# A conditioned attention and selective scan kernel: four exponential buffers, sample 1's projections queued ahead of sample 0's maxima, and a residual product that opens its sum

## The chip, the cores and the metric

The kernel runs on one core of a Trainium2 chip. Its time is the device time of one launch in microseconds, taken over several runs. The engines named below are the TensorE (PE), VectorE (DVE), ScalarE (ACT), GpSimd (POOL) and SyncE (SP, which issues nearly all DMAs). Each engine works through its own list of instructions in order and waits on semaphores for the others.

## What is computed

Two residual layers over x of 8 samples, 256 tokens, 256 channels. The first is attention with 16 heads of 16 channels, its weights modulated by a style vector:

```python
x = x + L0(x, q, k, v, w, u weights, cond)
x = x + L1(x, cond, ...)

# L0: x = layernorm(x * s1); q, k, v = projections, scaled by channel
attn = softmax(q @ k.T * 0.25)            # per head, 256 x 256
out  = (attn @ v) @ W.T * w_dc + v_flat @ U.T * u_dc

# L1: xr, gate = split(x @ W_in.T); xr + cond, causal conv of 4 taps, silu, layernorm -> xn
def step(h, ad, bd, xt, ct):              # 256 steps, state 16 x 512 per sample
    h = clip(h * ad + bd * xt, -10, 10)
    return h, ct @ h
y = ys + D * xn
return (y * silu(gate)) @ W_out.T
```

All inputs and the output are float32.

## The kernel before

The program is one list per engine, written out by hand, with a semaphore for each hand-over. There is no planner: the order in each engine's list is the order of the code.

**Attention.** `sample` on the TensorE runs once per sample b. Q and k are projected channels-first into banks 1 and 2 (`channels_of`, L694), copied out, and split by ScalarE and GpSimd into three bfloat16 parts (L480 to L487, L381, L385). SyncE's `stack` (L249, L259) writes the parts to memory and loads them back stacked, so that one matmul of 96 rows gives a float32-like product. A first pass of matmuls (`max_scores`, L713) gives each head's scores and the VectorE takes their row maxima (L1117). The maxima are transposed (L812), copied to bfloat16 (L514), and sent by a small DMA of the ScalarE's queue (L516) into row 96 of the stacked q. The second pass (`scores`, L723) has 97 rows, so it yields scores minus maxima, and the ScalarE takes exponentials (L522) out of banks 4 to 7, a head each, into `ex`. Heads go in four groups of four. For a group g, `weigh(.., False)` (L740) multiplies with v, `add_tiles` on the VectorE (L1135) adds the two halves of the exponentials into `esum`, and `weigh(.., True)` (L733) sums those over the partitions and raises `pv_done`. `attend` (L1141, L1143) divides for two groups at a time.

On the TensorE a sample's order is: maxima of heads 4 to 15, with the next sample's transposes (L686) and three projections between them at heads 4, 7 and 10; transposes of the maxima; output products of the previous sample (L758); scores 0, v transposes (L704), scores 1, weigh 0, scores 2, sums 0, weigh 1, scores 3, sums 1, weigh 2, sums 2, weigh 3, the next sample's first four maxima (`early_maxima`, which waits for the stacked loads), sums 3. Sample 0 has first its own projections, then four small matmuls L873 whose result the VectorE uses for weight gains (L1161 to L1165, `wgain`), for which the TensorE waits before `sample(0)`.

**Middle.** Input projection, convolution, layer norm, split of xn and of the scan's factors into bfloat16 parts, all by way of memory.

**Scan.** The 256 steps go in 16 tiles of 16, each of four groups of four. For step t one bfloat16 matmul (L951, `u_steps`) gives the increment in bank t % 4, and one VectorE instruction (L1315) adds it to the state and clips. For each group, `y_steps` (L962) contracts four states. The previous tiles' results are finished between them: `tile_transpose` (L972) after group 1, `tile_out` (L983) in two halves after group 3 and after group 0 of the next tile but one, the second half with the residual product x1 times identity (L987). The ScalarE copies y, the transposed y, x1 (`take_x1`, L645) and the output (`take_out`, L653). SyncE loads a tile's operands (L297, L305) when the slot's last increment is done, one tile before they are used, and stores the output (L329).

The lines on which the order rests:

```python
act.wait_ge(s["pv_done"], b * 4 + (g - 1))        # ScalarE, L521, before exp of group g
pe.wait_ge(s["wgain"], 1)                         # TensorE, L876, before sample 0
pe.wait_ge(s[f"ld_k{par}"], turn * 48 + 48)       # TensorE, L772, early_maxima
act.wait_ge(s["o_done"], r)                       # ScalarE, L644, before the copy of x1
```

Of the kernel before, what the change touches and what calls it, by code (L numbers as in the profile page):

```python
# [19 lines left out]
ALU = mybir.AluOpType  # L20
ACT = mybir.ActivationFunctionType
AX = mybir.AxisListType

P = 128
# [43 lines left out]
def build(nc, x_tok, xT, s1_row, condT, w5T, winT, wconv, bconv, ln_row, lnT, wxT, wxdt, wdtT, bdt_row, alog_row,  # L68
          woT, ident_d, mask8_d, out):
    with ExitStack() as ctx:  # L70
# [74 lines left out]
        mT = sb0("mT", [NH, S], BF16)  # L145
        ex = sb0("ex", [P, 2, 4, 512])
        esum = sb0("esum", [P, 2, 4, S])
# [307 lines left out]
        def _(act):  # L455
# [51 lines left out]
            def sample(b, par, last):  # L507
# [9 lines left out]
                for n in range(NH):  # L517
                    g = n // 4
                    act.wait_ge(s["st_done"], b * NH + (n + 1))
                    if n % 4 == 0 and not (isinstance(b, int) and b == 0 and g < 2):  # L520
                        act.wait_ge(s["pv_done"], b * 4 + (g - 1))  # L521
                    nc.scalar.activation(ex[:, g % 2, n % 4, :], bank[4 + n % 4][:, :], ACT.Exp, scale=SCALE)\  # L522
                        .then_inc(s["exp_done"], 1)
                    if n == 3 and not last:
                        take_v(b + 1, 1 - par, isinstance(b, int) and b == 0)
# [140 lines left out]
        def _(pe):  # L666
# [60 lines left out]
            def weigh(b, buf, g, sums):  # L727
# [10 lines left out]
                for t in range(HALVES):  # L738
                    for r in range(4):
                        mm(bank[2 * o][32 * r:32 * r + 32, 0:S],  # L740
                           vp[:, buf, t, 4 * o + r, 2 * par:2 * par + 2, :].rearrange("p a d -> p (a d)"),
                           ex[:, g % 2, r, t * S:(t + 1) * S], start=par == 0 and t == 0,
                           stop=par == 1 and t == HALVES - 1, skip_group_check=True)
# [32 lines left out]
            def sample(b, par, next_turn, first, last):  # L776
# [24 lines left out]
                for n in range(EARLY, NH):  # L801
                    if n == 4:
                        next_qkv(0)
# [64 lines left out]
            channels_of(2, 3, "vt_done")  # L868
            v_tokens(0)

            pe.wait_ge(s["ld_l1"], 16 * 11)
# [94 lines left out]
            def tile_transpose(r):  # L966
# [7 lines left out]
                ins.then_inc(s["yt_done"], 1)  # L974

            def tile_out(r, part):

                if part == 0:
                    pe.wait_ge(s["yg_ready"], r + 1)
                    if r >= 1:  # L980
                        pe.wait_ge(s["ob_ready"], r)
                for c in range(2 * part, 2 * part + 2):
                    mm(bank[7][:, 0:H], yg[:, c, :], wo[:, c, :], start=c == 0, stop=False, skip_group_check=True)  # L983
                if part == 1:
                    pe.wait_ge(s["x1s_ready"], r + 1)
                    for k in range(HT):
                        ins = mm(bank[7][:, k * P:(k + 1) * P], x1s[:, k, :], ident[:, :], start=False,  # L987
                                 stop=k == HT - 1, skip_group_check=True)
                    ins.then_inc(s["o_done"], 1)
# [3 lines left out]
            for i in range(R):  # L993
                for g in range(RG):
# [4 lines left out]
                    if i >= 1:  # L999
                        if g == 1:  # L1000
                            tile_transpose(i - 1)
                        elif g == 3:
                            tile_out(i - 1, 0)
                        elif g == 0 and i >= 2:
                            tile_out(i - 2, 1)
            tile_out(R - 2, 1)
            tile_transpose(R - 1)
            tile_out(R - 1, 0)
# [4 lines left out]
        def _(dve):  # L1013
# [107 lines left out]
            def sample(b, first, last, more):  # L1121
# [9 lines left out]
                def add_tiles(g):  # L1131
                    dve.wait_ge(s["exp_done"], b * NH + (4 * g + 4))
                    if not (first and g < 2):
                        dve.wait_ge(s["pv_done"], b * 4 + (g - 1))
                    v.tensor_tensor(esum[:, g % 2, :, :], ex[:, g % 2, :, 0:S], ex[:, g % 2, :, S:], ALU.add)\  # L1135
                        .then_inc(s["es_ready"], 1)
# [238 lines left out]
```

## Time and profile before

| | |
|---|---|
| median of 3 runs | 683.56 us (683.29 to 688.03) |
| the profiled execution | 684.64 us |
| its span, first to last instruction | 682.8 us |
| busy, share of the span | PE 73%, DVE 72%, ACT 35%, POOL 24% |
| chain that ended last | PE 35%, DVE 28%, ACT 15%, DMA 11% |
| largest lines of the chain | DVE scan step L1315 11%, ACT exponentials L522 8%, PE projections L694 6% |
| mean granted TensorE clock | 0.894 |

The span is the profiled execution's stretch from its first to its last instruction; its own time is 1.84 us more. A busy share is an average over stages of different kind, so it does not say what bounds any of them. The chain of waits is followed back from the last instruction, at each step to what released it. In a timeline row the first number is the start from the span's beginning, the second the time from the first to the last of the instructions that the row merges, x4 their count, and the bracket the engine's idle time ahead of them with what ended it. The granted clock is a share of 2.4 GHz: 0.5 is the lower of its two levels.

### The profile page before, as it was taken

What the parts mean: (1) busy time and instruction counts of PE and PEld (TensorE: products, weight loads), DVE (VectorE), ACT (ScalarE), POOL (GpSimd) and SP (SyncE); (2) the same over time, 40 slices, a digit from 0 to 9 for tenths busy, and PEclk for the clock granted to TensorE, in tenths of its full rate; (3) what the DMA queues carried; (4) which work ended last, traced back from release to release, by engine and by line L of the source; (5) the groups of instructions that cost most, each with busy time, mean ns of one, the idle gap of its engine ahead of it and who ended that gap; (6) DMA issues with size and microseconds to landing.
All of it is one profiled execution on the core that took longest, in us unless ns stands there. A gap on an engine that the chain in (4) does not pass through costs nothing.

```text
span 682.8 us, 8835 instructions
## 1 busy us (share of the span) xinstructions
PE 498.5 (73%) x3239; PEld 291.7 (43%) x3256; DVE 488.7 (72%) x807; ACT 239.3 (35%) x488; POOL 163.2 (24%) x176
## 2 busy tenths in 40 slices
PE   3558888888888886899996310036598898898896
PEld 3446455464645543478885210001133333333333
DVE  2825768586776858645667689737599999999994
ACT  2305445545454550447766355500011111111111
POOL 5302021020202100056000024400324334333331
PEclk9856999999999998999998555559799999999999
DMA  8743452706255270002100045796655755766720
GB/s 353 238 86 70 71 101 40 140 17 124 51 90 101 40 139 1 3 0 116 71 0 1 15 154 187 270 111 85 93 87 116 122 96 110 109 106 104 122 51 24
DMA packets 42214, 65.14 MB, mean 95 GB/s; under 512 B 18327, under 2 KB 33047, under 8 KB 39178
## 3 DMA queue, kind: packets, MB, share of 16 engines
q1 hardware_dynamic: 41130, 61.36, 43.5%
q0 software_dynamic: 784, 3.15, 1.1%
q8 instruction: 26, 0.43, 0.3%
q14 instruction: 18, 0.15, 0.1%
q10 hardware_dynamic: 256, 0.07, 0.0%
HBM read 41.88 MB, written 22.61 MB: 94 GB/s over the span
## 4 chain that ended last, share of the span: by engine, by line
PE 35%; DVE 28%; ACT 15%; DMA 11%; issue 5%; POOL 2%; SPq 1%; DVEq 0%; ACTq 0%
DVE zring L1315 11%; ACT ex L522 8%; PE bank L694 6%; DVE acc L1177 6%; DMA xst<-xs_d 5%; PE bank L983 5%; PE bank L713 4%; PE bank L962 4%; PE bank L951 4%; DVE mx L1117 3%; DMA qst<-mT 3%; ACT acc L562 2%; PE bank L750 2%; PE bank L723 2%; PE bank L733 2%
## 5 line engine op out<-in xcount | busy, mean ns | idle before, releaser
L1315 DVE CUSTOM_DVE_ANT_0 zring<-zring,bank,hi 128x512 f32<-128x512 f32 x192 | 143.6, 748 | 8.6 <-PE bank L951 1.9
L951 PE MATMUL bank<-xst,bst 128*128 128x512 bf16 x239 | 78.6, 398 | 79.4 <-DMA bst<-bd_d 46.7
L1117 DVE TENSOR_REDUCE mx<-bank 128x2 f32<-128x512 f32 x128 | 80.0, 684 | 23.3 <-PE bank L713 22.4
L951 PEld LDWEIGHTS bank<-xst,bst 128*128 128x128 bf16 x256 | 24.7, 98 | 137.0 <-issue 69.7
L522 ACT ACTIVATE ex<-bank 128x512 f32<-128x512 f32 x128 | 66.4, 619 | 41.9 <-PE bank L723 22.3
L962 PE MATMUL bank<-zring,cst 128*32 128x512 f32 x448 | 70.3, 623 | 1.7 <-DVE zlast L1315 1.7
L1135 DVE TENSOR_TENSOR esum<-ex 128x1024 f32<-128x1024 f32 x32 | 39.1, 1222 | 38.5 <-ACT ex L522 38.5
L381 POOL TENSOR_TENSOR qk<-qk,part 128x512 f32<-128x512 f32 x16 | 19.7, 1231 | 193.1 <-ACT part L484 193.1
L1177 DVE SCALAR_TENSOR_TENSOR acc<-xrp,wcv,acc 128x256 f32<-128x256 f32 x96 | 40.1, 480 | 29.3 <-ACT acc L562 28.7
L854 PE MATMUL bank<-xres,win 128*128 128x256 f32 x256 | 57.6, 382 | 1.2 <-ACT gateT L567 0.7
L723 PE MATMUL bank<-qst,kst 97*128 97x256 bf16 x256 | 44.3, 285 | 13.5 <-DMA qst<-mT 8.7
L694 PE MATMUL bank<-xnT,w 128*128 128x256 f32 x192 | 50.3, 410 | 4.8 <-ACT xnT L469 4.8
L854 PEld LDWEIGHTS bank<-xres,win 128*128 128x128 f32 x256 | 47.9, 190 | 8.5 <-issue 1.2
L629 ACT ACTIVATE ytk<-bank,ybias 128x512 f32<-128x512 f32 x15 | 10.3, 687 | 109.9 <-PE bank L962 109.9
L447 POOL TENSOR_TENSOR yg<-yT,gateT 128x128 f32<-128x128 f32 x60 | 29.2, 517 | 76.7 <-ACT yT L637 76.7
L713 PE MATMUL bank<-kst,qst 96*128 96x256 bf16 x256 | 38.5, 287 | 10.9 <-DMA kst<-qk_d 7.2
L410 POOL TENSOR_TENSOR xpart<-xrem,xpart 128x512 bf16<-128x512 f32 x16 | 20.7, 1310 | 100.2 <-ACT xpart L609 100.2
L1315 DVE CUSTOM_DVE_ANT_0 zring<-zlast,bank,hi 128x512 f32<-128x512 f32 x32 | 23.9, 748 | 27.8 <-PE bank L951 27.2
L694 PEld LDWEIGHTS bank<-xnT,w 128*128 128x128 f32 x192 | 37.6, 206 | 11.7 <-ACT xnT L469 6.6
L740 PE MATMUL bank<-ex,vp 128*32 128x256 f32 x512 | 34.5, 388 | 7.6 <-ACT ex L522 7.6
L983 PE MATMUL bank<-wo,yg 128*128 128x256 f32 x128 | 36.4, 411 | 1.0 <-DVE yg L1326 1.0
L723 PEld LDWEIGHTS bank<-qst,kst 97*128 97x128 bf16 x256 | 18.6, 100 | 40.5 <-ACT ex L522 26.1
(168 smaller groups left out, 773.1 us busy)
## 6 DMA issues: line engine op xcount, KB each, us to landing
qk_d<-part SPq DMA_DIRECT2D x64, 96.0 KB, 2.5
xs_d<-xpart SPq DMA_DIRECT2D x16, 384.0 KB, 2.6
xst<-xs_d SPq DMA_DIRECT2D x15, 384.0 KB
xn_d<-xc SPq DMA_DIRECT2D x16, 256.0 KB, 2.8
xtk<-xn_d SPq DMA_DIRECT2D x64, 64.0 KB
xst<-xs_d SPq DMA_DIRECT2D x15, 256.0 KB
qst<-qk_d SPq DMA_DIRECT2D x8, 384.0 KB, 4.7
kst<-qk_d SPq DMA_DIRECT2D x8, 384.0 KB, 8.0
```

The source lines that it names most:

```text
L522: nc.scalar.activation(ex[:, g % 2, n % 4, :], bank[4 + n % 4][:, :], ACT.Exp, scale=SCALE)\
L694: ins = mm(bank[bk][:, o * S:(o + 1) * S], w5[:, w, k, o * P:(o + 1) * P], xnT[:, k, :], start=k == 0, stop=k == HT - 1)
L713: ins = mm(bank[4 + n % 4][:, t * S:(t + 1) * S], qst[0:96, par, HEADS[n], t * P:(t + 1) * P], kst[0:96, par, HEADS[n], :], start=True, st ...
L723: ins = mm(bank[4 + n % 4][:, t * S:(t + 1) * S], kst[0:97, par, HEADS[n], t * P:(t + 1) * P], qst[0:97, par, HEADS[n], :], start=True, st ...
L854: ins = mm(bank[4 + c // 2][:, (c % 2) * S:(c % 2 + 1) * S], win[:, k, c * P:(c + 1) * P], xres[:, k, bass.ds(b * S, S)], start=k == 0, st ...
L951: mm(bank[t % 4][:, :], bst[:, slot, t % RS, :], xst[:, slot, t % RS, :], start=True, stop=True)\
L962: ins = mm(bank[4 + i % 2][32 * k:32 * k + 32, :], cst[:, i % 2, 32 * (4 * g + k):32 * (4 * g + k) + 32], zst[(4 * g + k) % ZR], start=g = ...
L983: mm(bank[7][:, 0:H], yg[:, c, :], wo[:, c, :], start=c == 0, stop=False, skip_group_check=True)
L1117: v.tensor_reduce(mx[:, :, HEADS[n]:HEADS[n] + 1], bank[4 + n % 4][:, :].rearrange("p (t k) -> p t k", t=HALVES), AX.X, ALU.max)\
L1135: v.tensor_tensor(esum[:, g % 2, :, :], ex[:, g % 2, :, 0:S], ex[:, g % 2, :, S:], ALU.add)\
L1177: ins = v.scalar_tensor_tensor(acc[:, c, :], xrp[:, c, k:k + S], wcv[:, c, k:k + 1], acc[:, c, :], ALU.mult, ALU.add)
L1315: v._custom_dve(bass.dve_ops.TENSOR_ADD_SAT, out=zst[t % ZR], in0=zst[(t - 1) % ZR], in1=bank[t % 4][:, :], s0=hi[:, t:t + 1], s1=0.0).the ...
```

## The change

Three things are changed. The buffer of exponentials `ex` has four slots in place of two, and the ScalarE waits for the sums of group g of the sample before in place of those of group g - 2. The TensorE's transposes and projections of sample 1 move from between sample 0's maxima to ahead of L873, in the order q, k, v. The residual product becomes a function of its own, is issued after group 2 and opens the accumulation in bank 7, which the output product's two halves continue and close; for the last tile it stands ahead of the last transposes.

```diff
--- before.py
+++ after.py
@@ -143,7 +143,7 @@
         vp = sb0("vp", [P, 2, HALVES, NH // 2, 4, HD])
         mx = sb0("mx", [P, HALVES, NH])
         mT = sb0("mT", [NH, S], BF16)
-        ex = sb0("ex", [P, 2, 4, 512])
+        ex = sb0("ex", [P, 4, 4, 512])
         esum = sb0("esum", [P, 2, 4, S])
         rec = sb0("rec", [P, HT, S])
         attT = sb0("attT", [P, HT, S])
@@ -517,9 +517,9 @@
                 for n in range(NH):
                     g = n // 4
                     act.wait_ge(s["st_done"], b * NH + (n + 1))
-                    if n % 4 == 0 and not (isinstance(b, int) and b == 0 and g < 2):
-                        act.wait_ge(s["pv_done"], b * 4 + (g - 1))
-                    nc.scalar.activation(ex[:, g % 2, n % 4, :], bank[4 + n % 4][:, :], ACT.Exp, scale=SCALE)\
+                    if n % 4 == 0 and b >= 1:
+                        act.wait_ge(s["pv_done"], b * 4 + (g - 3))
+                    nc.scalar.activation(ex[:, g, n % 4, :], bank[4 + n % 4][:, :], ACT.Exp, scale=SCALE)\
                         .then_inc(s["exp_done"], 1)
                     if n == 3 and not last:
                         take_v(b + 1, 1 - par, isinstance(b, int) and b == 0)
@@ -739,7 +739,7 @@
                     for r in range(4):
                         mm(bank[2 * o][32 * r:32 * r + 32, 0:S],
                            vp[:, buf, t, 4 * o + r, 2 * par:2 * par + 2, :].rearrange("p a d -> p (a d)"),
-                           ex[:, g % 2, r, t * S:(t + 1) * S], start=par == 0 and t == 0,
+                           ex[:, g, r, t * S:(t + 1) * S], start=par == 0 and t == 0,
                            stop=par == 1 and t == HALVES - 1, skip_group_check=True)
 
             def project_att(b):
@@ -799,7 +799,9 @@
                 if first:
                     early_maxima(b, par, 0)
                 for n in range(EARLY, NH):
-                    if n == 4:
+                    if first:
+                        pass
+                    elif n == 4:
                         next_qkv(0)
                         next_qkv(1)
                     elif n in (7, 10):
@@ -868,6 +870,15 @@
             channels_of(2, 3, "vt_done")
             v_tokens(0)
 
+            transpose_xn(1, True)
+            pe.wait_ge(s["xnT_ready"], 2)
+            pe.wait_ge(s["q_in"], 1)
+            channels_of(0, 1, "q_done")
+            pe.wait_ge(s["k_in"], 1)
+            channels_of(1, 2, "k_done")
+            pe.wait_ge(s["v_in"], 1)
+            channels_of(2, 3, "vt_done")
+
             pe.wait_ge(s["ld_l1"], 16 * 11)
             for c in range(CT):
                 ins = mm(bank[6][:, c * NS:(c + 1) * NS], wxd[:, c * P:(c + 1) * P], wdt[:, :], start=True, stop=True)
@@ -973,19 +984,23 @@
                                               ident[:, :])
                 ins.then_inc(s["yt_done"], 1)
 
+            def tile_residual(r):
+
+                pe.wait_ge(s["x1s_ready"], r + 1)
+                if r >= 1:
+                    pe.wait_ge(s["ob_ready"], r)
+                for k in range(HT):
+                    mm(bank[7][:, k * P:(k + 1) * P], x1s[:, k, :], ident[:, :], start=k == 0, stop=False,
+                       skip_group_check=True)
+
             def tile_out(r, part):
 
                 if part == 0:
                     pe.wait_ge(s["yg_ready"], r + 1)
-                    if r >= 1:
-                        pe.wait_ge(s["ob_ready"], r)
                 for c in range(2 * part, 2 * part + 2):
-                    mm(bank[7][:, 0:H], yg[:, c, :], wo[:, c, :], start=c == 0, stop=False, skip_group_check=True)
+                    ins = mm(bank[7][:, 0:H], yg[:, c, :], wo[:, c, :], start=False, stop=c == CT - 1,
+                             skip_group_check=True)
                 if part == 1:
-                    pe.wait_ge(s["x1s_ready"], r + 1)
-                    for k in range(HT):
-                        ins = mm(bank[7][:, k * P:(k + 1) * P], x1s[:, k, :], ident[:, :], start=False,
-                                 stop=k == HT - 1, skip_group_check=True)
                     ins.then_inc(s["o_done"], 1)
 
             pe.wait_ge(s["ybias_ready"], 1)
@@ -999,11 +1014,14 @@
                     if i >= 1:
                         if g == 1:
                             tile_transpose(i - 1)
+                        elif g == 2:
+                            tile_residual(i - 1)
                         elif g == 3:
                             tile_out(i - 1, 0)
                         elif g == 0 and i >= 2:
                             tile_out(i - 2, 1)
             tile_out(R - 2, 1)
+            tile_residual(R - 1)
             tile_transpose(R - 1)
             tile_out(R - 1, 0)
             tile_out(R - 1, 1)
@@ -1132,7 +1150,7 @@
                     dve.wait_ge(s["exp_done"], b * NH + (4 * g + 4))
                     if not (first and g < 2):
                         dve.wait_ge(s["pv_done"], b * 4 + (g - 1))
-                    v.tensor_tensor(esum[:, g % 2, :, :], ex[:, g % 2, :, 0:S], ex[:, g % 2, :, S:], ALU.add)\
+                    v.tensor_tensor(esum[:, g % 2, :, :], ex[:, g, :, 0:S], ex[:, g, :, S:], ALU.add)\
                         .then_inc(s["es_ready"], 1)
 
                 def attend(o):
```

## Rows read from the trace of the kernel before

**Rows 1.** Timeline, samples 0 and 1: start us, us, instructions [idle before <-releaser].

```profile
...
72.77 2.06 ACT L522 ACTIVATE ex<-bank 128x512 f32<-128x512 f32 x4 [2.38 <-PE bank L733]
...
102.29 1.05 PE L740 MATMUL bank<-ex,vp 128*32 128x256 f32 x16
102.60 2.06 ACT L522 ACTIVATE ex<-bank 128x512 f32<-128x512 f32 x4 [1.15 <-PE bank L733]
...
105.83 1.75 DVE L1141 RECIPROCAL rec<-bank 128x256 f32<-128x256 f32 x1
...
107.96 1.21 DVE L1135 TENSOR_TENSOR esum<-ex 128x1024 f32<-128x1024 f32 x1
...
108.93 1.05 PE L713 MATMUL bank<-kst,qst 96*128 96x256 bf16 x8
...
```

**Rows 2.** Stretch: length, busy PE, PEld, DVE, ACT, POOL; clock, DMA share, GB/s.

```profile
...
536.90:671.00 134.10, 119.44 (x656) 45.46 (x664) 124.69 (x167) 20.61 (x42) 50.34 (x74) 1.00 0.59 99
...
```

**Rows 3.** Who waited for whom, scan from tile 2: us, times, longest.

```profile
...
DVE zring L1315 <- PE bank L951: 13.1, 16, 5.9
...
```

**Rows 4.** Busy time by engine before sample 0's maxima.

```profile
...
34.00:48.00 14.00, 6.10 (x25) 4.86 (x26) 4.20 (x13) 1.25 (x3) 0.00 (x0) 0.50 0.61 109
...
```

**Rows 5.** Timeline, start of sample 0.

```profile
...
35.09 1.89 PE L873 MATMUL bank<-wdt,wxd 16*128 16x16 f32 x8
...
38.58 0.28 DVE L1165 TENSOR_SCALAR lnb_rep<-ones,lnt 128x128 f32<-128x128 f32 x1
...
44.14 1.87 PE L713 MATMUL bank<-kst,qst 96*128 96x256 bf16 x8 [7.17 <-DMA kst<-qk_d]
...
47.55 3.78 PE L694 MATMUL bank<-xnT,w 128*128 128x256 f32 x8 [0.69 <-ACT xnT L469]
...
52.40 2.53 PE L694 MATMUL bank<-xnT,w 128*128 128x256 f32 x8
...
55.42 1.89 PE L694 MATMUL bank<-xnT,w 128*128 128x256 f32 x8
...
57.57 3.68 DVE L1117 TENSOR_REDUCE mx<-bank 128x2 f32<-128x512 f32 x6 [0.50 <-PE bank L713]
...
```

**Rows 6.** Chain of waits, samples 1 and 7: start us, us, what.

```profile
...
93.80 2.60 DMA qst<-mT
...
273.42 1.80 DMA qst<-mT
...
```

**Rows 7.** Loads of sample 2's keys: KB each, us to landing; first and last start.

```profile
...
kst<-qk_d SPq DMA_DIRECT2D x1, 128.0 KB, 8.9
L259 SPq DMA_DIRECT2D kst<-qk_d x3: 418/421/423, 98.5 to 99.4; - x3
...
```

**Rows 8.** Chain of waits in one steady tile.

```profile
...
534.86 1.06 PE bank L983 x4
535.92 0.45 PE bank L987 x4
...
536.93 0.76 DVE zring L1315
```

**Rows 9.** Timeline of the same tile, group 2.

```profile
...
539.34 0.41 ACT L645 ACTIVATE x1s<-xres 128x256 f32<-128x256 f32 x1
...
540.41 1.06 PE L962 MATMUL bank<-zring,cst 128*32 128x512 f32 x8
...
```

**Rows 10.** One load of a tile: chain of waits, then timeline.

```profile
...
579.89 13.50 DMA xst<-xs_d
...
593.93 1.21 PE L951 MATMUL bank<-xst,bst 128*128 128x512 bf16 x4 [0.93 <-DMA xst<-xs_d]
...
```

**Rows 11.** Timeline after the last scan step.

```profile
...
675.32 0.60 PE L972 MATMUL bank<-ident,ytk 128*128 128x128 f32 x4
...
675.80 0.41 ACT L645 ACTIVATE x1s<-xres 128x256 f32<-128x256 f32 x1
...
676.90 1.99 PE L983 MATMUL bank<-wo,yg 128*128 128x256 f32 x8 [0.97 <-DVE yg L1326]
...
```

## The prediction

> **What bounds the kernel now.** I read the stages first (the page's slices, then busy time by stretch), then the chain of waits, then the timeline around each edited place. Until about 297 us the kernel is attention over eight samples; a steady sample takes 29.8 us. In one, the ScalarE stops twice: the exponentials of head group 2 begin 1.15 us late, released by the TensorE's sum matmul L733, and those of group 3 in the same way at 102.60 + 2.06 + 1.15 = 105.81 [rows 1]. From 454 us the scan runs on the VectorE, 16 steps a tile. In steady tiles (536.9 to 671 us) it is busy 124.69 of 134.10 us [rows 2]; it is the bound, with one stop per tile: 14 stops of some 0.38 us where a gap is otherwise 0.03. The wait row's 13.1 us are 5.9 (a load, at tile 2), 1.9 (one slow-clock group in tile 1) and 5.3 in these 14 [rows 3]. At the start the TensorE waits 7.2 us for sample 0's stacked keys, at a granted clock of 0.50, the 1.2 GHz level [rows 4, 5].
>
> **Part 1, sample 1's projections first.** *Removed* from sample 0's maxima: four transposes, three projections of eight matmuls. *Added* in the wait: they start where L873 does now, at 35.09 [rows 5]; sample 1's normalised rows are there by then. Transposes 1.1, hand-over and copy 0.7: the first projection starts at 36.9. In sample 0 now, after the idle wait, the three took 3.78, 2.53 and 1.89 us [rows 5]: the low clock, the change, the high one. I take the same: done at 45.1. *Now late*: L873 stands behind them, 1.89 at the low clock and about 1.0 at the high one (I take 1.4), the VectorE's weight gains follow it (36.98 to 38.86, 1.9 us), and the TensorE waits for these before the first maxima. So the maxima start at 45.1 + 1.4 + 1.9 = 48.4, with hand-overs 48.5, and not at 44.14: 4.3 us later. But nothing interrupts them: 16 reductions at 0.61 us, the VectorE's own pace, are 9.8 us, so they end at 48.5 + 0.6 + 9.8 = 58.9 against 57.57 + 3.68 = 61.25. Gain 2.4. Bounds: all at the low clock (3 x 3.78 and 1.89) costs 3.6 us more, a loss of 1.2; all at the high one gains 3 more. Memory: sample 1's casts end at about 48 instead of 59.9, so its stack goes out early, and its loads land near 65 instead of 77, well before the 74 at which they are wanted. Their price is that the row of maxima, 8 KB on the ScalarE's queue, now crosses them. It took 2.60 us beside the write half of a stack and 1.80 with the queues quiet (sample 7) [rows 6]; no row has it beside the load half. I charge 0.2, nearest to those two; the other bound is that it waits for the loads to end, 65.6 - 62.4 = 3.2. The Trainium skill (DMA: Bandwidth & Descriptors, "Queues, rings and completion order") says that each DMA engine takes turns between queues packet by packet; by it the charge stays near 0.2, by one common line it would be 3.2. Part 1: **-2.2**.
>
> **Part 2, four exponential buffers.** The pair of buffers made group g wait for the sums of g-2, which the TensorE issues behind the scores of g. With four, exp of group 2 starts at 101.5 when group 1 ends. Group 3 needs its scores, queued behind the weighing of group 1 (102.29 + 1.05 = 103.3) [rows 1]: it starts at 103.7, 2.1 earlier. *Next late*: the VectorE. Its sum of group 2 ends at 101.5 + 2.06 + 1.23 = 104.8, then reciprocal and product (1.75 + 0.42), so the sum of group 3 starts at 107.0 instead of 107.96 [rows 1]. And the next sample's first maxima, at 108.93 now, need the stacked keys: the last of three loads is issued at 99.4 and lands 8.9 us later, at 108.3 [rows 7]. That wait takes the removed one's place. Sample 1's gain is 0.6, not 2.1. The same difference for the six samples that have such loads ahead (1 to 6) is 0.6, 1.0, 0.45, 0.5, 0.65, 0.2; less 0.1 each for the hand-over (44.0 landed, 44.14 begun) they give 2.8. The stack's start moves with the sample's own projections, so the gains add up. Sample 0 has no such limit (its successor's loads are early): its groups 2 and 3 stop 2.4 and 1.1 us [rows 1]; the VectorE's sums limit it: 1.6. Sample 7 has no loads ahead: 0.95, by the VectorE again. Part 2: **-5.35**. Bounds: nothing in samples 1 to 6 if loads land 0.5 later (-2.55); 0.95 in every one if they land sooner (-8.2).
>
> **Part 3, the residual product first.** Per tile, behind the output matmuls at the tile's group 0 stand two products with the identity: 0.45 us on the chain [rows 8]. In this group the TensorE has 1.00 + 1.06 + 0.45 and two u matmuls (0.45) between a scan step and the step that needs them, and the VectorE waits 0.39. Without the 0.45 it has the same work as in group 3, which stops nobody. The 0.35 is less than the 0.45 taken out, so the stop goes whole: 14 x 0.35 = 4.9. *Where they land*, group 2: the copy of x1 ends at 539.34 + 0.41 = 539.75, before this group's y matmuls begin at 540.41 [rows 9], and the output's copy-out is 3 us past. So neither wait bites, and 0.45 is less than the 0.60 of transposes that group 1 carries without a stop. SyncE and GpSimdE get nothing moved; the output's store is issued 0.45 earlier. *Next late*: a tile's loads, issued when the slot is free and wanted one tile later. In one of 12 tiles the last landed 13.5 us after its issue, and the TensorE began 0.93 late [rows 10]. There the VectorE still did not stop, with 0.2 us left. A tile shorter by 0.35 eats that, so I charge 0.5 over all tiles; bounds 0 and the full 4.9. *Tail*: the last residual now stands ahead of the last transposes. It needs x1's last copy, which the ScalarE makes after tile 14's copy-out: 675.80 + 0.41 less the 0.45 = 675.8. The transposes begin at 676.3 instead of 675.32, the last output matmuls 0.95 later than 676.90, with 0.45 less behind them [rows 11]: +0.5. Part 3: -4.9 + 0.5 + 0.5 = **-3.9**.
>
> **Sum.** -2.2 - 5.35 - 3.9 = -11.45. The profiled execution took 684.64 (span 682.8 and 1.84 around it): 673.2. The median of the runs, 683.56, stands 1.08 below it: **672.1**.
>
> **Rivals.**
> (a) *The scan becomes bound by its loads.* DMA engines are busy 0.59 on average [rows 2], and the tail of each load runs on a few. If these are already full for a 12.88 us tile, the stop at group 0 turns into one at the load: 4.9 comes out as nothing, the tail's 0.5 stays: 683.56 - 7.55 + 0.5 = 676.5. For it: the late load. Against: 11 of 12 loads came before they stopped anyone, with no growing lateness. The same skill page ("Why a DMA increments its semaphore by 16 and not by 1") has each copy use as many engines as divide its rows; by my estimate from it the busiest engines carry 108 KB a tile where the mean is 85, so 1.27 times the mean load, and would have room. No row shows single engines. Chance 0.13.
> (b) *The front does not pay*: projections all at the low clock, or the row of maxima behind the loads. Part 1 comes out at +1.2 or +1.0 instead of -2.2: 675.5. Chance 0.15.
> (c) *Attention stays bound by its loads*: keys land 0.5 us later and samples 1 to 6 give nothing: 674.9; with the front failing too, 678.2. Chance 0.10.
> (d) *Slower*: loads fall behind in the scan. The one place is the load wait at a tile's first u matmul. Early in the scan a load took 21 us and stopped the VectorE 5.9 [rows 3]. If the store and xn loads, now closer to the tile's loads, bring that back, it decides from two tiles on (2 x 5.9 = 11.8 eats the gain); with four, 683.56 - 11.45 + 23.6 = 695.7. Against: those 21 us had two tiles' loads and small-row stores in line, which the change does not bring. Chance 0.04.
> (e) *The edits do little*: exp of group 3 is held by the TensorE's queue as before, and the projections only move the wait. Then part 3 alone: 679.7. Against: in the timeline L733 alone stands between the end of one group and the start of the next. Chance 0.05.
>
> **How the numbers follow.** The forecast has 0.53. A measurement of this kernel can tell about 1%, 6.8 us, so the line is 676.7. The forecast, (b), (c) without the front and most of (a) lie below it. Range 667.5 to 678.5: down to the forecast with 0.95 in every sample and a quicker front (668), up to (a) and the double case of (c). Above it are (d), (e) and mixtures, below it little. Faster by over 1%: 0.82; within 1%: 0.13; slower: 0.05.
>
> **What would show it.** Projections of sample 1 between 36 and 46 us; maxima of sample 0 from 48.5 without a break; first scores at 62.5 instead of 65.0. No wait of the exponentials for L733; instead L713 released by the kst load, and a sample of 29.3 us. Steady tiles of 12.55 us, DVE idle before L1315 from L951 near 8 us in all instead of 13.1, the residual line after group 2's y matmuls. After the last scan step, 11.2 us to the end where it was 10.8. Wrong if: samples stay at 29.8 us; tiles stay at 12.88 with a load as releaser; the first maxima start after 50.

## The result, and the profile after

The changed kernel takes 675.83 us (median of 4 runs, 672.83 to 678.42) where the kernel before takes 683.42 (4 runs, 683.03 to 688.03). The ratio is 0.9862, 95% interval 0.9823 to 0.9901: 1.4% faster. Forecast: 672.1, range 667.5 to 678.5. The profiled execution took 672.83 (span 671.0, 1.83 around it), against 684.64 (span 682.8). It is the fastest of the four, so each step below is also held against a second trace of the same kernel (run e4). Every ratio in this document leaves out the few runs that lie over 1.5% above the fastest of the same kernel, so it can differ a little from the quotient of two medians.

| Step | before | forecast | trace after | second trace |
|---|---|---|---|---|
| first scores of sample 0 | 64.98 | 62.5 | 63.94 | 64.75 |
| first scan step | 454.58 | 447.0 | 446.19 | 448.91 |
| from there to the end of the last step | 217.42 | 213.0 | 213.40 | 218.02 |
| from there to the end of the span | 10.8 | 11.3 | 11.4 | 11.5 |

The forecast's 11.3 is 10.8 and its charge of 0.5; among its signs the prediction has 11.2.

**The start.** The timeline of TensorE and VectorE (start us, us, engine, line, operation, tiles, count, [idle before <- releaser]):

```profile
36.70 7.18 PE L694 MATMUL bank<-xnT,w 128*128 128x256 f32 x24 [0.69 <-ACT xnT L469]
43.81 1.06 PE L884 MATMUL bank<-wdt,wxd 16*128 16x16 f32 x8
48.37 1.86 PE L713 MATMUL bank<-kst,qst 96*128 96x256 bf16 x8 [3.51 <-issue]
...
48.99 9.66 DVE L1135 TENSOR_REDUCE mx<-bank 128x2 f32<-128x512 f32 x16 [0.72 <-PE bank L713]
```

The three projections fill what was the wait for the keys ([rows 5]), and the sixteen reductions run as one piece. They end at 58.65 where the forecast had 58.9. Two errors of the working cancel here: the projections and L884 (L873 before the change) were done at 44.87 and not at 46.5, and the weight gains behind them took 3.4 us and not 1.9. The first of the gains stands beside two casts of the GpSimd:

```profile
44.88 2.26 POOL L385 TENSOR_TENSOR part<-qk,part 128x512 bf16<-128x512 f32 x2
45.99 1.23 DVE L1183 TENSOR_SCALAR lnb_rep<-ones,lnt 128x128 f32<-128x128 f32 x1
47.30 0.27 DVE L1183 TENSOR_SCALAR lnb_rep<-ones,lnt 128x128 f32<-128x128 f32 x1
```

In the chain of waits the row of maxima, 2.60 us before at sample 1 ([rows 6]) and 2.6 at sample 0, takes for sample 0

```profile
59.74 4.15 DMA qst<-mT
```

**One sample.** Who waited for whom from 60 to 300 us (us in total, times, longest):

```profile
ACT ex L522 <- PE bank L723: 26.0, 16, 3.1
...
PE bank L713 <- DMA kst<-qk_d: 8.2, 6, 1.9
```

Before, the first of these was 22.3, 8, 3.2 and the second did not exist. The row `ACT ex L522 <- PE bank L733: 19.6, 16, 2.4` of before is gone, and the stacked keys are waited for six times. In the timeline, where [rows 1] have 102.60, 105.83, 107.96 and 108.93:

```profile
100.28 2.07 ACT L522 ACTIVATE ex<-bank 128x512 f32<-128x512 f32 x4 [0.28 <-PE bank L723]
...
101.54 1.76 DVE L1159 RECIPROCAL rec<-bank 128x256 f32<-128x256 f32 x1 [0.28 <-PE bank L733]
...
103.67 1.22 DVE L1153 TENSOR_TENSOR esum<-ex 128x1024 f32<-128x1024 f32 x1
...
105.11 1.03 PE L713 MATMUL bank<-kst,qst 96*128 96x256 bf16 x8 [1.48 <-DMA kst<-qk_d]
```

The exponentials of group 3 follow those of group 2 with no break but the 0.28 of their scores. The VectorE's sum then ends at 104.89, and the TensorE stands until 105.11 for the keys; the chain has that load as `96.00 8.98 DMA kst<-qk_d`. Samples 1 to 6, each from its first scores to the next sample's, take 28.3 to 29.7 us instead of 29.8.

**The scan.** The same table from 507 to 671 us, and a steady tile's residual, which now stands behind group 2's y matmuls ([rows 3, 8]):

```profile
DVE zring L1333 <- PE bank L962: 5.7, 2, 4.1
```

```profile
544.03 1.06 PE L973 MATMUL bank<-zring,cst 128*32 128x512 f32 x8
545.02 0.71 PE L993 MATMUL bank<-ident,x1s 128*128 128x128 f32 x4
545.57 0.88 PE L962 MATMUL bank<-xst,bst 128*128 128x512 bf16 x3
```

The 14 stops of 0.38 are gone and a tile takes 12.53 us instead of 12.88. From tile 3 on two stops are left, both in tile 4 of the scan. In the timeline of the VectorE, and in the chain:

```profile
507.57 0.75 DVE L1333 CUSTOM_DVE_ANT_0 zring<-zlast,bank,hi 128x512 f32<-128x512 f32 x1 [4.06 <-PE bank L962]
...
512.36 2.31 DVE L1333 CUSTOM_DVE_ANT_0 zring<-zring,bank,hi 128x512 f32<-128x512 f32 x3 [1.68 <-PE bank L962]
```

```profile
491.08 13.34 DMA xst<-xs_d
...
508.29 1.87 PE bank L973 x8
```

The TensorE waited for this tile's load, and its granted clock fell while it did: the eight y matmuls behind it took 1.87 us for the steady tile's 1.06, and that is the second stop. Before, no VectorE stop stood at the first step of tile 4.

**The tail** ([rows 11]), after the last scan step at 659.59:

```profile
663.41 0.71 PE L993 MATMUL bank<-ident,x1s 128*128 128x128 f32 x4 [0.78 <-ACT x1s L645]
...
663.96 0.60 PE L983 MATMUL bank<-ident,ytk 128*128 128x128 f32 x4
...
665.53 1.99 PE L1001 MATMUL bank<-wo,yg 128*128 128x256 f32 x8 [0.97 <-DVE yg L1344]
```

The transposes wait behind the residual, which waits for the ScalarE's copy.

### The profile page after: what moved, and what is told of

Same layout as the page of the kernel before. It is cut to its first block, busy times and chain, and to the rows that moved or that the text cites. A ratio compares the mean times of both kernels' runs of the same rounds, so it can differ in the third digit from the quotient of the medians.

```text
span 671.0 us, 8832 instructions
## 1 busy us (share of the span) xinstructions
PE 495.6 (74%) x3238; PEld 291.5 (43%) x3256; DVE 490.5 (73%) x807; ACT 238.7 (36%) x488; POOL 163.2 (24%) x176
## 4 chain that ended last, share of the span: by engine, by line
DVE 33%; PE 32%; DMA 17%; ACT 8%; issue 6%; POOL 2%; SPq 1%; DVEq 0%; ACTq 0%
DVE zring L1333 12%; DMA kst<-qk_d 8%; PE bank L694 6%; DVE acc L1195 6%; DMA xst<-xs_d 4%; PE bank L1001 4%; PE bank L962 4%; PE bank L973 4%; PE bank L713 4%; DVE mx L1135 3%; DMA qst<-mT 3%; ACT acc L562 2%; PE bank L750 2%; PE bank L723 2%; ACT xrp L557 2%
## 5 line engine op out<-in xcount | busy, mean ns | idle before, releaser
L1135 DVE TENSOR_REDUCE mx<-bank 128x2 f32<-128x512 f32 x128 | 79.7, 684 | 12.4 <-PE bank L713 11.5
L522 ACT ACTIVATE ex<-bank 128x512 f32<-128x512 f32 x128 | 65.6, 645 | 26.1 <-PE bank L723 26.0
L381 POOL TENSOR_TENSOR qk<-qk,part 128x512 f32<-128x512 f32 x16 | 19.6, 1230 | 186.7 <-ACT part L484 186.7
L1153 DVE TENSOR_TENSOR esum<-ex 128x1024 f32<-128x1024 f32 x32 | 39.1, 1222 | 28.8 <-ACT ex L522 28.3
L713 PE MATMUL bank<-kst,qst 96*128 96x256 bf16 x256 | 41.2, 296 | 14.4 <-DMA kst<-qk_d 8.2
L723 PE MATMUL bank<-qst,kst 97*128 97x256 bf16 x256 | 39.7, 282 | 12.5 <-DMA qst<-mT 9.8
L447 POOL TENSOR_TENSOR yg<-yT,gateT 128x128 f32<-128x128 f32 x60 | 29.2, 515 | 74.7 <-ACT yT L637 74.7
L713 PEld LDWEIGHTS bank<-kst,qst 96*128 96x128 bf16 x256 | 23.5, 101 | 31.9 <-issue 14.9
L973 PE MATMUL bank<-zlast,cst 128*32 128x512 f32 x64 | 35.7, 642 | 0.0
```

The lines of the kernel that those rows point to most:

```text
L522: nc.scalar.activation(ex[:, g, n % 4, :], bank[4 + n % 4][:, :], ACT.Exp, scale=SCALE)\
L713: ins = mm(bank[4 + n % 4][:, t * S:(t + 1) * S], qst[0:96, par, HEADS[n], t * P:(t + 1) * P], kst[0:96, par, HEADS[n], :], start=True, st ...
L723: ins = mm(bank[4 + n % 4][:, t * S:(t + 1) * S], kst[0:97, par, HEADS[n], t * P:(t + 1) * P], qst[0:97, par, HEADS[n], :], start=True, st ...
L973: ins = mm(bank[4 + i % 2][32 * k:32 * k + 32, :], cst[:, i % 2, 32 * (4 * g + k):32 * (4 * g + k) + 32], zst[(4 * g + k) % ZR], start=g = ...
L1135: v.tensor_reduce(mx[:, :, HEADS[n]:HEADS[n] + 1], bank[4 + n % 4][:, :].rearrange("p (t k) -> p t k", t=HALVES), AX.X, ALU.max)\
L1153: v.tensor_tensor(esum[:, g % 2, :, :], ex[:, g, :, 0:S], ex[:, g, :, S:], ALU.add)\
```

## The experiments

Each ratio is to the kernel before on the same chip, whose own runs there spread from 679 to 690 us. The first four ran together, then e5 to e8, then e9 to e11.

### Each part alone, and the whole again

e1 is the kernel before with part 1 alone:

```diff
-                    if n == 4:
+                    if first:
+                        pass
+                    elif n == 4:
...
+            transpose_xn(1, True)
+            pe.wait_ge(s["xnT_ready"], 2)
+            pe.wait_ge(s["q_in"], 1)
+            channels_of(0, 1, "q_done")
...
             pe.wait_ge(s["ld_l1"], 16 * 11)
```

> The kernel before with only sample 1's projections moved ahead. My account of the changed kernel's trace: first scores of sample 0 at 64.0 instead of 65.0 us, since the row of maxima took 4.15 us beside sample 1's loads where it took 2.60 before. If that is the whole of part 1, this kernel is 1.0 us faster (682.4) and its maxima row again lands late. The rival (the row is late by chance in that one profile) gives 2.4: 681.0. A second rival, that what moves the loads in time also moves the load waits of the scan, gives any value between 680 and 685 with the difference lying after 440 us.

Measured: 687.01, ratio 1.000 (0.9963 to 1.0037), so no gain, where the account of the trace gave 1.0 us.

e2 is part 2 alone:

```diff
-    ex = sb0("ex", [P, 2, 4, 512])
+    ex = sb0("ex", [P, 4, 4, 512])
...
-                        act.wait_ge(s["pv_done"], b * 4 + (g - 1))
+                        act.wait_ge(s["pv_done"], b * 4 + (g - 3))
```

> The kernel before with only the four buffers of exponentials. Theory: samples 1 to 6 are then bound by the landing of the next keys, so 0.2 to 1.0 us each comes out, sample 0 about 1.2 to 1.6 (its successor's loads land at 77.0, before the 77.5 at which they are wanted), sample 7 0.95: 5 us, 678.4. Rival, samples bound by their own engines: 1 us or more in each, 8 us, 675.4. Rival, no gain since group 3 waits in the TensorE's queue: 683.

Measured: 681.42, ratio 0.9931 (0.9895 to 0.9967), samples of 28.8 to 29.7 us.

e3 is part 3 alone:

```diff
                             tile_transpose(i - 1)
+                        elif g == 2:
+                            tile_residual(i - 1)
                         elif g == 3:
```

> The kernel before with only the residual product moved. Theory: the 14 stops of 0.35 us go (4.9), the tail costs 0.6, so steady tiles take 12.54 instead of 12.88 and the time is 679.1 if no load stops the scan more than before. Rival: the shorter tiles run into their loads and the gain is 0 to 2 us (681 to 684), with new stops of the VectorE at a tile's first step in the first tiles, as one of 4.1 us in the changed kernel's trace. This one also tells whether the runs spread (672.8 to 678.4 in the changed kernel, 683.0 to 683.6 before): by the load theory they spread here, in the two kernels above they don't.

Measured: 682.77, ratio 0.9955 (0.9928 to 0.9982). Of the VectorE's stops from 507 us on, this row is left:

```profile
DVE zring L1322 <- PE bank L951: 1.4, 1, 1.4
```

e4 is the changed kernel once more, with no edit, beside the parts.

> The changed kernel once more, for its spread and for a second trace. Theory: the execution differs from run to run only in how long loads stop the scan in its first tiles (12.6 us in the first trace); so this trace's time minus the first trace's 672.83 equals the difference of those stops, and everything before 440 us agrees within 1 us. Rival: the samples' key loads vary, so the difference lies before 280 us. If the three parts add, this kernel's gain is the sum of the gains of the three kernels above; if they share a limit it is smaller.

Measured: 679.64, ratio 0.9898 (0.9865 to 0.9931). By the intervals' middles the parts give 0, -4.7 and -3.1 us, together -7.8; the whole gives -7.0 here. So the parts add up within their uncertainty, and the one that falls short is the first. The theory that executions differ only in the scan's stops holds in part: of the 7.4 us between the two traces' spans 2.7 lie ahead of the first scan step and 4.6 in the scan. Nor is the spread new: the kernel before has 680.05 to 690.07 on this chip.

Where part 1's gain goes is seen in its own trace. Its row of maxima is `59.74 4.21 DMA qst<-mT` and sample 1's first scores begin at 94.41 instead of 96.45, as the scan does at 452.58 instead of 454.58: 2.0 us won, half of it (0.97) at sample 0's first scores and half (1.06) right behind them. The scan then takes 221.59 us instead of 217.42, with a stop of 6.32 us at tile 4. The trace of e4 has one there too, of 4.12 us, and 17.7 us of stops in all. So in these traces what is won ahead of the scan is taken back in it. The scan of one kernel differs by 4.6 us from one execution to another, so one trace shows this only in part; e1's ratio agrees with it.

### The row of maxima and the tail

e5: sample 1's stack is loaded only when the row has landed, and the last transposes go ahead of the last residual.

```diff
                 sp.wait_ge(s["pw"], b * (16 * NH // HT) + 16 * NH // HT)
+                if b == 1:
+                    sp.wait_ge(s["m_row"], 16)
...
+            tile_transpose(R - 1)
             tile_residual(R - 1)
-            tile_transpose(R - 1)
```

> The changed kernel with two repairs. First, sample 1's loads are issued only when sample 0's row of maxima has landed. If that row was late because the loads shared the DMA engines, it now lands 2.6 us after its issue instead of 4.15 and the first scores begin near 62.4 instead of 63.9 us; sample 1's first maxima may then wait up to 0.5 us for their keys (issued 62.4, landed 73.5, wanted near 73.6). Rival, that the ScalarE queue's DMA was late for another reason: still 4 us, and sample 1 late by as much as before. Second, the last tile's residual goes behind the last transposes: these begin 0.95 us earlier and the residual hides beside the VectorE's last gate product, so the stretch from the last scan step to the end is 10.4 us instead of 11.4 (10.8 before the change). Together 2.2 to 2.5 us off the changed kernel: 0.9865 of the time before where the changed kernel has 0.990.

Measured: 675.76, ratio 0.985 (0.9807 to 0.9892); this overlaps e4's interval, so the two repairs are read from the trace. In the timeline, SyncE's loads now come behind the row, and the view of DMA issues has its landing (SPq and ACTq are the DMA issues of SyncE and ScalarE):

```profile
59.57 0.60 ACTq L518 DMA_DIRECT2D qst<-mT  x1
...
61.54 1.25 SPq L261 DMA_DIRECT2D qst<-qk_d  x3
62.21 1.91 PE L725 MATMUL bank<-qst,kst 97*128 97x256 bf16 x8
```

```profile
qst<-mT ACTq DMA_DIRECT2D x1, 8.0 KB, 1.9
```

The row lands in 1.9 us instead of 4.15, and the first scores stand at 62.21, 1.7 earlier. Not all of this is kept: the low clock lasts longer behind them, and the third group of scores stands at 67.86 for 68.97 (69.78 in the second trace), 1.1 earlier. In the changed kernel the last of these loads were issued at 55.6 at the latest. Held back they still serve: this trace first uses the keys at 73.98, with no wait. The tail, from the last scan step at 667.08 to the end at 677.0, is 9.9 us instead of 11.4.

### The stops of the scan: a store of small rows

In tile 1 of the scan SyncE issues six stores of 1024 rows of 32 bytes each, ahead of tile 4's load. In the changed kernel's timeline:

```profile
473.39 13.41 SPq L313 DMA_DIRECT2D bd_d<-bpart  x6
486.85 0.68 SPq L329 DMA_DIRECT2D out<-ob  x1
487.57 2.57 SPq L323 DMA_DIRECT2D xtk<-xn_d  x4
490.18 1.22 SPq L297 DMA_DIRECT2D xst<-xs_d  x3
```

e6 puts them three tiles later:

```diff
-                if i == 1:
+                if i == 4:
                     store_b(1)
```

> The changed kernel with the second store of the scan's split factors (six DMAs of 1024 rows of 32 bytes each) issued three tiles later. Theory: these small rows fill the DMA engines when tile 4's load is issued, and that load's lateness is the stop of 4.1 us at the first step of tile 4; so this stop goes and one like it comes at tile 7. Rival: the early loads are late for reasons of their own and the stop stays at tile 4 with no new one at tile 7. The time stays within 2 us of the changed kernel's either way.

Measured: 683.46, ratio 0.994 (0.9904 to 0.9976). It was to stay within 2 us of the changed kernel; by the ratios it is some 3 us above e4, with intervals that overlap. The stop moves with the store, from tile 4 to tile 7, and grows:

```profile
555.80 0.75 DVE L1333 CUSTOM_DVE_ANT_0 zring<-zlast,bank,hi 128x512 f32<-128x512 f32 x1 [10.31 <-PE bank L962]
```

```profile
536.52 16.34 DMA xst<-xs_d
```

Here the load is issued in time and lands late. In the second trace of the changed kernel (e4) the chain runs through SyncE's own issues instead: two of the six stores take 7.73 and 4.02 us to issue, and tile 4's load stands behind them in SyncE's list.

e7 issues one of the six in each of the tiles 0 to 5:

```diff
-                if i == 1:
-                    store_b(1)
+                if i < len(PAIRS):
+                    store_b(1, i)
```

> The changed kernel with those six DMAs issued one a tile in tiles 0 to 5 instead of all in tile 1. By the theory of e6 each tile's load then meets 1024 small rows and not up to 6144, about 3 us of it, within the slack of 1.5 us or a little over: the stop of 4.1 us at tile 4 goes or shrinks to under 1, and 3 to 5 us come off where it occurred (all three traces of kernels with stops at tile 4 or its neighbours). Rival: every one of six tiles stops a little and the sum is the same.

Measured: 675.55, ratio 0.9831 (0.979 to 0.9872). An issue now takes 0.38 us of SyncE, not 13.41 for six:

```profile
477.74 0.38 SPq L315 DMA_DIRECT2D bd_d<-bpart  x1
```

The scan takes 208.75 us where the changed kernel's two traces have 213.40 and 218.02, and no stop is left from tile 4 on. e6 and e7 together show the cause of that stop: the six stores in one piece.

The spread has a price of its own, which e9 (below, with the same edit) shows. Tile 8's load may be issued only when all six stores have landed. The last of them, issued in tile 5, lands 12.39 us later; the load is issued behind it, and the scan stops at tile 8:

```profile
528.33 12.39 DMA bd_d<-bpart
```

```profile
555.93 0.75 DVE L1337 CUSTOM_DVE_ANT_0 zring<-zlast,bank,hi 128x512 f32<-128x512 f32 x1 [2.42 <-PE bank L966]
```

With the 0.99 behind it this costs e9 3.4 us. In e7 the load is held in the same way, to 544.68, and nothing stops.

### The keys

e8 issues each of the q and k loads from sample 2 on with its first 4 rows only (of 48, 32 or 16), so its output is another one; the TensorE's and ScalarE's work is the same.

```diff
+                        rows = run * HD if first else 4
-                        sp.dma_start(st[at:at + run * HD, par, :, :], ...)
+                        sp.dma_start(st[at:at + rows, par, :, :], ...[0:rows])
```

> The changed kernel with the stacked q and k loads of samples 2 to 7 cut to their first 4 rows (of 48, 32 and 16), so the scores are computed from old rows; only the time tells. Theory: samples 1 to 6 are bound by the landing of the next sample's keys. Then the wait of L713 for the load goes and a sample takes 28.3 us (limit: the VectorE's sum of group 3, 0.96 us earlier than before the change) instead of 28.6 to 29.7; five to six samples give 4 to 6 us. Rival: the samples are bound by the TensorE and VectorE anyway, 29.2 us each as now.

Measured: 671.52, ratio 0.979 (0.9742 to 0.9837; 2 runs). Samples 1 to 5 take 28.42 to 28.46 us each, where the changed kernel's take 28.6 to 29.7 (mean 29.2), and the wait of L713 for kst is gone from the table. What the TensorE waits for now is

```profile
PE bank L734 <- DVE esum L1154: 3.6, 8, 1.3
```

So the loads' landing did take the removed wait's place, and the VectorE's sum is next in line.

### Repairs together

e9 has the edits of e5 and e7 in one kernel.

> The changed kernel with all three repairs: sample 1's loads held until the row of maxima has landed (1.7 us in the trace of that kernel), the last residual behind the last transposes (1.5), the small-row store one DMA a tile (the stop at tile 4, 4 to 6 us). If they add: 7 us under the changed kernel, near 0.980 of the time before (changed kernel 0.990). Rival: the early scan's loads make up for it elsewhere: 0.984, as either repair alone.

Measured: 670.4, ratio 0.979 (0.975 to 0.9829), where 0.980 was expected if the repairs add. Its trace has the row at 1.9 us, 10.0 us behind the last step, and a scan of 209.77 with the stop at tile 8.

e10 is the changed kernel in another order: group 3's sums and the transposes of sample b+2 go ahead of the early maxima that need the keys, and the VectorE's last product ahead of its reductions.

```diff
                 weigh(b, par, 3, False)
+                weigh(b, par, 3, True)
+                if b < B - 2:
+                    transpose_xn(b + 2, False)
                 if not last:
                     early_maxima(b + 1, 1 - par, next_turn)
-                weigh(b, par, 3, True)
...
                     elif n == 4:
-                        next_qkv(0)
                         next_qkv(1)
...
+                attend(1)
                 if not last:
                     dve.wait_ge(s["mt_done"], b + 1)
                     maxima(b + 1, 0, EARLY)
-                attend(1)
```

> The changed kernel, but the sums of group 3 and the next but one sample's transposes stand ahead of the first maxima, which need the keys; the VectorE divides the second half before it takes those maxima. Theory: the changed kernel's samples are bound by the loop keys' load, first maxima, transposes, projections, store, load; and the wait of 0.7 to 1.9 us for the keys, just before the projections, is where the clock fell in two of six traces, which made one sample 3 us longer. With the transposes ahead of the wait this loop is cut: projections begin about 1.5 us earlier, a sample takes 27.7 instead of 29.2 us, six samples give 9 us (667 where the changed kernel has 676), and no sample of 32 us occurs. Rival: the keys are not the limit, but the VectorE or the TensorE's own work is: a sample stays within 0.3 us of 29.2.

Measured: 677.29, ratio 0.9875 (0.9828 to 0.9922). Samples 1 to 5 take 28.81 to 28.90 us in its trace, not the 27.7 of my theory. The table of waits, and one sample's timeline:

```profile
PE bank L733 <- DVE esum L1154: 10.5, 8, 1.3
```

```profile
105.71 1.22 DVE L1154 TENSOR_TENSOR esum<-ex 128x1024 f32<-128x1024 f32 x1
106.98 0.64 PE L733 MATMUL bank<-esum,half_ones 128*32 128x256 f32 x8 [1.31 <-DVE esum L1154]
```

With the keys out of the way the TensorE stands for the VectorE's sum instead: the wait changes its name and keeps its size (10.5 us here; in the changed kernel 8.2 for the keys and 1.6 for this sum). By the ratios alone e10 can't be told from the changed kernel.

e11 joins e9 and e10.

> The two kernels above in one. If the parts add: 7 + 9 = 16 us under the changed kernel, about 0.967 of the time before. If the reordering gives nothing: 0.980, as the three repairs alone.

Measured: 667.86 (664.76 to 669.82), ratio 0.9746 (0.9707 to 0.9784). It is the fastest, 16.4 us below the kernel before on its chip. It lies between its two expectations (0.967 and 0.980), and its interval overlaps e9's from 0.975 to 0.9784, so a gain of the reordering on top of e9 is likely but not shown.

## Why the prediction was right, and where it was not

**Part 1** was to give 2.2 us at sample 0's first scores and gave 1.0 there in the one trace and 0.2 in the other (63.94 and 64.75 for 64.98). The maxima began at 48.37 for 48.5, which is luck. The clock rose sooner than taken (projections 7.18 us for 8.2, L884 1.06 for 1.4), and this covered a term that was too small: the weight gains took 3.4 us for 1.9. Their first two instructions, beside the GpSimd's casts, took 0.81 and 1.23 us instead of 0.25 and 0.28, in every trace with part 1; that the casts are the cause was not tested. Over the traces the maxima begin between 48.20 and 49.60.

The term that failed is *the row of maxima*: I charged 0.2 for crossing the key loads, between bounds of 0 and 3.2. It took 4.03 to 4.71 us in the seven traces that have it beside them, where 2.60 was the most before: 1.4 to 2.1 us. The charge came from the two nearest rows. The Trainium skill (DMA: Bandwidth & Descriptors, "Queues, rings and completion order") has each DMA engine take turns between queues packet by packet, and by the prediction's reading of it the row would have been nearly free. The seven traces don't bear this out, and one common line, 3.2 late, is too much; they stand between. In e5, e9 and e11, in which no load is in flight, the row takes 1.9. So the crossing loads are the cause, though not how the engines share.

A gain that no term had made up for part of this. The low clock ends sooner behind sample 0's first scores. Before, in the timeline from 66 us on:

```profile
69.38 1.72 PE L740 MATMUL bank<-ex,vp 128*32 128x256 f32 x16
...
71.03 1.05 PE L723 MATMUL bank<-qst,kst 97*128 97x256 bf16 x8
```

and after:

```profile
67.97 1.07 PE L740 MATMUL bank<-ex,vp 128*32 128x256 f32 x16
...
68.97 1.05 PE L723 MATMUL bank<-qst,kst 97*128 97x256 bf16 x8
```

From the first to the third group of scores it is 6.05 us before, 6.05 and 6.06 in e3 and e2, and 4.99 to 5.03 in e1 and the changed kernel's two traces (5.65 in e5, where the row is early). With this 1.0 part 1 gave 2.1, 1.2 and, in e1, 2.0 us ahead of the scan. So its size came out near the forecast by errors that offset each other, and its mechanism was right only in part.

**Part 2** was to give 5.35 us and did, as far as can be told. Both named successors were found: the landing of the keys' loads (e8 removes it) and behind it the VectorE's sum (e8 and e10). From the first scores to the first scan step the changed kernel's traces gained 7.35 and 5.44, of which 1.0 is part 1's clock: 6.3 and 4.4; e2 alone gained 5.4 in its trace and 4.7 by its ratio. Samples 1 to 6, forecast at 2.8 together, gave 4.5, 2.75 and 3.7 in these three traces, and single samples between 0.04 and 1.47. A load's landing decides and changes from one sample to the next (8.1 to 9.4 us in the first trace), so half a microsecond per sample is not to be had from one execution. That 5.35 is met in the mean is in part luck.

**Part 3**, steady tiles: 0.35 us in each, as said; the 14 stops are gone, and behind tile 4 none came at a load in either trace (e9's at tile 8 has another source). So rival (a) did not come. The tail cost 0.6 for the forecast's 0.5, and e5 shows it as needless: transposes first gives 1.5 back. *Early tiles* are the other term that failed. I charged 0.5 for all loads together and kept the pattern of before. The forecast of 213.0 for the scan met 213.40 in the first trace, since the stops at tiles 1 and 2 shrank (4.39 to 2.62, 5.93 to 2.85) while those of tile 4 (4.06 and 1.68) came in, which is luck; the second trace had them all (4.43, 4.88, 2.31, 4.12, 1.97), and its scan was 218.02. This is rival (d)'s mechanism at about a quarter of its price (4.12 and 1.97 of 23.6). Its source is the store of small rows, which I had set aside because the change does not touch it; e6 and e7 show it. The prediction put the 1.9 of low clock in tile 1; it stands at 494.87 in tile 2, right behind the 5.93. In the changed kernel's traces, too, each stop at tile 2 or 4 has one of 1.4 to 2.3 behind it, so a late load costs more than its own wait.

**The sum.** The first trace ended at 672.83, where the forecast for an execution was 673.2. The medians stand at 675.8 and, on the later chip, at -7.0 us from before, 4.4 short of the forecast. The row of maxima is 1.2 to 1.9 of this, of which the clock gave 1.0 back; the larger part lies in the early scan, where executions differ by 4.6 us. The subtraction of 1.08 for the median had no ground either: it took the difference of one execution from its neighbours as a property of the kernel.

**What stays open.** A stop of over 4 us at the first step of tile 4 stands in all six traces that have part 1 and the stores in tile 1, and in none of the three without part 1 (0, 0.88 and 1.36). The stores are its cause; why part 1 brings it out was not found. It goes with a shorter stop at tile 2 in some pairs (5.93 and 0 before, 2.85 and 4.06 after) but not in others (4.12 and 1.36 in e3, 4.59 and 6.32 in e1).

## What to carry to other kernels

When a wait is taken out, price what ends the next one, and treat a DMA's landing as a spread rather than a number: it caps the gain and makes it vary. A transfer that is moved costs where it lands: look for the small transfers on the critical path that it now crosses, and hold it back if it has time to spare. Many small rows in one piece delay loads whole stages later, so spread them over several stages, but let the last of them land before its reader has to be issued (e9's stop at tile 8).

## What the runs showed of the hardware

**The clock fell after a wait of 1.5 us, at times.** In two of the traces with a wait for the keys, once each, the TensorE dropped to its 1.2 GHz level right after it had stood for the keys. The timeline of e7, with the same group of eight matmuls 30 us earlier above it:

```profile
166.94 1.99 PE L696 MATMUL bank<-xnT,w 128*128 128x256 f32 x8 [0.69 <-ACT xnT L471]
...
193.40 1.03 PE L715 MATMUL bank<-kst,qst 96*128 96x256 bf16 x8 [1.50 <-DMA kst<-qk_d]
...
196.62 3.78 PE L696 MATMUL bank<-xnT,w 128*128 128x256 f32 x8 [0.69 <-ACT xnT L471]
```

and its busy time by stretch (length, busy PE, its weight loads PEld, DVE, ACT and POOL, granted clock, DMA share, GB/s):

```profile
161.00:172.00 11.00, 8.93 (x81) 6.39 (x74) 9.79 (x13) 3.11 (x7) 1.15 (x1) 1.00 0.09 16
191.00:202.00 11.00, 8.81 (x56) 5.80 (x45) 7.84 (x11) 2.06 (x4) 0.00 (x0) 0.69 0.02 4
```

This sample took 32.30 us instead of 29.2. In e5 the same came after a wait of 1.65 us (a sample of 32.49), while one of 1.49 us a sample earlier left the clock at 1.00, as did one of 1.88 us in the changed kernel (221.87, the next eight matmuls 1.99). So did one of 2.00 us in e5 itself (225.07). So the length of the wait alone does not decide it, and what else does is open. In e3 the clock fell at the very end instead: the last output matmuls, behind an idle 0.98 us, took 3.68 us where the changed kernel has 1.99 behind 0.97, and the stretch behind the last step was 13.1 us for 11.4. Traces without this wait (e8, e10, e11) never show it. A wait can cost more than its length, 3 us here beside its 1.5.

**Six small-row stores can hold their queue.** Alone one issue takes SyncE 0.38 us. Six in a row took 12.75 to 16.56 us in tile 1 or 4 of the scan (e6, before), right behind a tile's loads, and SyncE issued nothing else in that time. The same six for the first half of the rows, ahead of the scan, took 3.50 us in every trace:

```profile
434.42 3.50 SPq L313 DMA_DIRECT2D bd_d<-bpart  x6
```

So it is not their number alone; what else it takes was not tested.
